# Three expert chunks moved from the recurrence to the heads of the first sequence's attention

## The chip, the cores and the metric

The kernel runs on one core of a Trainium2 chip. Five engines matter here: TensorE (PE) does matrix products and transposes, VectorE (DVE), ScalarE (ACT, activation functions and copies) and GpSimd (POOL) do elementwise work, and SyncE issues transfers. The metric is the time of one execution in device microseconds. The kernel before takes 3566.51 us, the median of three runs (3561.74 to 3568.43).

## The reference, cut to what matters

A small language model tower over 16 sequences of 256 tokens, width 256. Two layers, each an attention-like part and an expert part. Layer 0: token embedding, a linear recurrence with a channel mix, then a mixture of eight experts. Layer 1, where the change lies:

```
# recurrence (per channel, over time)
k = x @ Wk.T; r = x @ Wr.T; v = r
q = max(pp, u + k); y = (exp(pp-q)*a + exp(u+k-q)*v) / (exp(pp-q)*b + exp(u+k-q))
h = h + (sigmoid(r) * y) @ Wo.T
# attention, 16 heads of 16, causal, then four experts
h = rms(x) ; q, k, v = heads(h @ wq.T), ... ; attn = softmax(mask(q k^T / 4))
x = x + (attn v) @ wo.T            # first 64 columns set to zero
xf = rms(x); wts = top-2 of softmax(xf @ gate_w.T)
o0 = gelu(xf @ e0_up.T) @ e0_down.T
o1 = silu(xf @ e1_w1.T) * (xf @ e1_w2.T) @ e1_down.T
o2 = gelu(gelu(gelu(xf @ e2_l1.T) @ e2_l2.T) @ e2_l3.T) @ e2_l4.T
o3 = gelu(gelu(xf @ e3_down.T) @ e3_up.T) @ e3_out.T
out = x + sum of wts[e] * o_e      # first 64 columns set to zero
```

## The kernel before, in words

Three phases follow each other: a (layer 0's embedding and recurrence), b (layer 0's experts) and c (layer 1). Only phase c is touched. It works on eight tiles of 512 tokens, two sequences each. Values that need more than bf16 are split into a high and a low bf16 half, and each product is three passes (high by high, low weight by high, high by low).

Each engine has a queue that runs in order. All four compute engines walk the same list of steps, `ORDER_C`, and each engine does its own part of a step; semaphores connect the parts. The *front* of a tile is:

- f2, the key and receptance products of the recurrence, and their copies on ScalarE; r2, the end of the router of the tile before, on VectorE.
- A0/A1: VectorE makes the exponents of channel half 0 or 1. R0/R1: ScalarE takes the exponentials (L1276), VectorE runs the scans and the division (L1461 to L1483). Z0/Z1: ScalarE writes the high half of the result z (L1287), VectorE the low half (L1490).
- f5: TensorE's output product (first row L1739, after z), VectorE's addition and statistics, GpSimd's reciprocal roots (L1204 to L1208). g5: VectorE applies the normalization (L1398). f6: TensorE transposes, ScalarE and GpSimd split.
- Q0 to Q3, K0 to K3, T0 to T3: the q, k, v products, their norms, and the transposed stacks (L1801). M0/M1: maxima of the scores per sequence; N0/N1: their negative, transposed (L1325).
- S0 to S15 and V0 to V15: the heads of the first sequence. S: TensorE's scores (L1846 to L1850) into one of two banks, ScalarE's exponential (L1333), VectorE's high half (L1580), and the low half on GpSimd (L1223) or, for every third head, on VectorE (L1583). V: TensorE's weighted values (L1867 to L1870). V of a head stands three heads behind its S; the weights have four buffers (PB). S16 to V31 are the second sequence. O0/O1: ScalarE copies the result (L1340).

The *back* of a tile is its router and its experts, cut into 42 chunks: in the order of `WORK`, four each of e2_l1, e0_up, e2_l2 and e0_down, two of e3_down, four each of e2_l3, e3_up, e2_l4, the gated expert e1, e3_out and e1_down. An *up* chunk is six matmuls of 512 columns (contraction 256) or twelve (contraction 512, as e2_l2 and e2_l3), two gelus on ScalarE (L1367, L1368) and one low half on GpSimd (L1233). It may start when the gelus of the up chunk two before it are done (`free`). A *down* chunk is twelve matmuls of 192 columns (L1956) and, for the last of four, an update of h on VectorE (L1716). A number in `ORDER_C` stands for that many chunks, the next in line, and `heads_order(b, fill)` puts `fill[h]` chunks behind head h.

The experts of tile t run in the same walk as the front of tile t+1. So the first tile's front runs without chunks, seven walks have both (`Fori` holds five of them), and the last tile's experts run alone.

ScalarE's functions come in table sets. Where the function of the next activation is in another set than the last, the program has an ACT_TABLE_LOAD before it; gelu is in another set than the exponential, copies load nothing.

Of the kernel before, what the change touches and what calls it, by code (L numbers as in the profile page):

```python
# [935 lines left out]
def heads_order(b, fill, lag=3):  # L936

    steps = []
    for h in range(HEADS + lag):
        if h < HEADS:  # L940
            steps.append("S%d" % (b * HEADS + h))
        if h >= lag:
            steps.append("V%d" % (b * HEADS + h - lag))
        if h in fill:
            steps.append(str(fill[h]))
    return " ".join(steps)


ORDER_C = " ".join((
    "f2 A0 r2 R0 A1 8 Z0 1 R1 6 Z1 f5 3 g5 2 f6 1 Q0 Q1 K0 2 T0 K1 1 T1 1 M0 1 N0",  # L950
    heads_order(0, {8: 1}), "O0",
    "Q2 3 Q3 K2 1 T2 K3 1 T3 1 M1 1 N1",
    heads_order(1, {4: 1, 9: 1, 14: 1}), "O1 1 f13 f0 1 g13 b0 1 g0 1 y0 1 b1 f1 r1"))

# [1114 lines left out]
```

## Time and profile before

| | |
|---|---|
| median of three runs | 3566.51 us (3561.74 to 3568.43) |
| the profiled execution, its time | 3563.41 us |
| its span, first to last instruction | 3561.6 us |
| busy in the span: TensorE | 2902.6 us (81%) |
| VectorE | 2051.2 us (58%) |
| ScalarE | 1674.7 us (47%) |
| GpSimd | 791.4 us (22%) |
| mean granted TensorE clock | 0.919 |

The profile is of one execution. Its page cuts the span into 40 slices; phase c fills the last 19 of them, where the TensorE digits are 6 to 8 and ScalarE's 3 to 5. The timeline lists instructions with start, duration, engine, line and what they write and read. A bracket at its end says how long the engine had been idle, and whose instruction ended the wait. The names `c_...` are tiles of phase c; `xT_hi` and `xT_lo` are memory of an earlier phase that phase c uses for its own buffers (in the heads `xT_lo` holds the weights in f32 and `xT_hi` their halves). A granted clock of 1.00 is 2.4 GHz, 0.50 is 1.2 GHz.

### The profile page before, as it was taken

How to read it: one execution, taken by the hardware profiler on the slowest of the kernel's cores; microseconds unless marked ns; L12 is line 12 of the kernel's file. 1: busy time of each engine (PE TensorE's matmuls, PEld its weight loads, DVE VectorE, ACT ScalarE, POOL GpSimd, SP SyncE). 2: the span in 40 equal slices, each digit the busy share in tenths (PEclk: the TensorE clock that was granted, in tenths of full speed). 3: DMA queues.
4: the chain of work that ended last, by engine and by line, in shares of the span. 5: the costliest groups of instructions: out<-in, count | busy, mean ns of one | idle time of the engine just before them, and what ended most of it. 6: DMA issues, size and time to landing. Idle time of an engine off the chain costs nothing. (4 is left out here: it accounts for less than half of the span.)

```text
span 3561.6 us, 59951 instructions
## 1 busy us (share of the span) xinstructions
PE 2902.6 (81%) x21952; PEld 1880.1 (53%) x21952; DVE 2051.2 (58%) x3989; ACT 1674.7 (47%) x2804; POOL 791.4 (22%) x813
## 2 busy tenths in 40 slices
PE   4877759999999999999994667777777777777778
PEld 2544446666666666666662444445353444445354
DVE  6777734444444444444446576665766676675762
ACT  2544535555555555555442445443544545453543
POOL 4545320000000000000000143432333243333333
PEclk8989879999999999999997789998998988898999
DMA  1000010000000000000000000000000000000000
GB/s 60 7 12 12 1 48 23 21 20 18 18 18 21 19 18 18 18 22 18 0 0 0 1 1 1 7 1 8 1 1 7 1 7 1 7 1 7 1 1 13
DMA packets 17448, 40.58 MB, mean 11 GB/s; under 512 B 2944, under 2 KB 7040, under 8 KB 17152
## 3 DMA queue, kind: packets, MB, share of 16 engines
q1 hardware_dynamic: 15744, 34.11, 3.1%
q0 software_dynamic: 1536, 4.20, 0.4%
q8 instruction: 110, 1.80, 0.2%
q14 instruction: 58, 0.48, 0.0%
HBM read 34.10 MB, written 4.19 MB: 11 GB/s over the span
## 5 line engine op out<-in xcount | busy, mean ns | idle before, releaser
L864 DVE TENSOR_TENSOR b_glo<-b_f,b_ghi 128x512 bf16<-128x512 f32 x512 | 354.1, 692 | 715.5 <-ACT b_ghi L807 715.4
L806 ACT ACTIVATE b_f<-b_up,b_b 128x512 f32<-128x512 f32 x512 | 352.5, 688 | 609.7 <-PE b_up L901 583.3
L915 PE MATMUL b_down<-b_W_hi,b_ghi 128*128 128x256 bf16 x2048 | 558.4, 273 | 17.4 <-DVE b_glo L864 17.4
L915 PE MATMUL b_down<-b_W_lo,b_ghi 128*128 128x256 bf16 x2048 | 558.2, 273 | 0.0
L915 PE MATMUL b_down<-b_W_hi,b_glo 128*128 128x256 bf16 x2048 | 558.2, 273 | 0.0
L1233 POOL TENSOR_TENSOR c_hid_lo<-c_g,c_hid_hi 128x512 bf16<-128x512 f32 x208 | 266.1, 1289 | 673.2 <-ACT c_hid_hi L1368 395.3
L807 ACT ACTIVATE b_ghi<-b_up,b_b 128x512 bf16<-128x512 f32 x512 | 349.2, 682 | 0.0
L901 PE MATMUL b_up<-xT_hi,b_W_hi 128*128 x1024 | 305.4, 380 | 13.1 <-DVE b_W_lo L819 13.1
L1190 POOL TENSOR_TENSOR c_frs<-c_fmv,eps 128x4 f32<-128x4 f32 x8 | 1.6, 197 | 1394.1 <-DVE c_fmv L1391 1394.1
L901 PE MATMUL b_up<-xT_hi,b_W_lo 128*128 x1024 | 305.1, 380 | 0.0
L901 PE MATMUL b_up<-xT_lo,b_W_hi 128*128 x1024 | 305.0, 379 | 0.0
L915 PEld LDWEIGHTS b_down<-b_W_hi,b_ghi 128*128 128x128 bf16 x2048 | 200.3, 98 | 92.6 <-issue 35.1
L915 PEld LDWEIGHTS b_down<-b_W_lo,b_ghi 128*128 128x128 bf16 x2048 | 200.4, 98 | 58.0
L915 PEld LDWEIGHTS b_down<-b_W_hi,b_glo 128*128 128x128 bf16 x2048 | 200.4, 98 | 23.2
L1367 ACT ACTIVATE c_g<-c_back 128x512 f32<-128x512 f32 x176 | 105.1, 597 | 216.6 <-PE c_back L1732 186.8
L1223 POOL TENSOR_TENSOR xT_hi<-xT_lo,xT_hi 128x384 bf16<-128x384 f32 x176 | 170.1, 978 | 158.6 <-DVE xT_hi L1580 158.6
L1333 ACT ACTIVATE xT_lo<-c_front 128x384 f32<-128x384 f32 x256 | 123.7, 491 | 113.3 <-PE c_front L1850 98.4
L901 PEld LDWEIGHTS b_up<-xT_hi,b_W_lo 128*128 128x128 bf16 x1024 | 100.4, 98 | 121.4 <-issue 1.0
L901 PEld LDWEIGHTS b_up<-xT_lo,b_W_hi 128*128 128x128 bf16 x1024 | 100.3, 98 | 121.1 <-issue 0.6
L1580 DVE CAST xT_hi<-xT_lo 128x384 bf16<-128x384 f32 x256 | 106.6, 435 | 87.1 <-ACT xT_lo L1333 83.9
L1560 DVE TENSOR_REDUCE c_mx<-c_front 128x2 f32<-128x512 f32 (+1 forms) x192 | 125.3, 688 | 47.1 <-PE c_front L1822 42.4
L1739 PE MATMUL c_front<-WC_hi,c_xhi 128*128 128x256 bf16 (+2 forms) x256 | 68.7, 359 | 97.7 <-DVE c_xlo L1490 33.7
(351 smaller groups left out, 6764.9 us busy)
## 6 DMA issues: line engine op xcount, KB each, us to landing
b_stage<-in_WP SPq DMA_DIRECT2D x59, 383.0 KB, 3.1
out<-h SPq DMA_DIRECT2D x8, 512.0 KB, 2.9
xT_hi<-in_WA SPq DMA_DIRECT2D x4, 512.0 KB, 6.0
xT_lo<-in_WA SPq DMA_DIRECT2D x3, 512.0 KB, 9.2
b_b<-in_b SPq DMA_DIRECT2D x1, 1024.0 KB, 5.2
b_ghi<-in_WP SPq DMA_DIRECT2D x2, 383.0 KB, 6.7
b_glo<-in_WP SPq DMA_DIRECT2D x2, 383.0 KB, 6.9
a_emb<-in_emb,idx POOLq DMA_INDIRECT x32, 2.8
```

What stands on the lines that cost most here:

```text
L806: act.activation(f[:, k % 4, :], ub[k % 4][:, :], ACT.Gelu, bias=b1[par][:, k:k + 1])
L807: act.activation(ghi[:, k, :], ub[k % 4][:, :], ACT.Gelu, bias=b1[par][:, k:k + 1]).then_inc(g_hi.sem, 1)
L864: dve.tensor_tensor(glo[:, k, :], f[:, k % 4, :], ghi[:, k, :], ALU.subtract).then_inc(g_lo.sem, 1)
L901: m = pe.matmul(ub[k % 4][:, :], wp[par][:, q * H0 + k * P:q * H0 + (k + 1) * P], xp[:, bass.ds(t * TT + q * N, TT)], start=(n == 0 and q ...
L915: m = pe.matmul(ob[s // 2][:, (s % 2) * D:(s % 2 + 1) * D], xp[:, k, s * P:(s + 1) * P], wp[par][:, w], start=(k == 0 and n == 0 and s % 2 ...
L1223: pool.tensor_tensor(pl[:, n % PB, :], pf[:, n % PB, :], ph[:, n % PB, :], ALU.subtract).then_inc(p_lo_pool.sem, 1)
L1233: pool.tensor_tensor(hid_lo[dst][:, k, :], g[:, h % 2, :], hid_hi[dst][:, k, :], ALU.subtract).then_inc(lo_ready.sem, 1)
L1333: act.activation(pf[:, n % PB, :], fb[n % 2][:, 0:3 * P], ACT.Exp).then_inc(p_f.sem, 1)
L1367: act.activation(g[:, h % 2, :], bb[2 + u % 2][:, :], ACT.Gelu)
L1560: dve.tensor_reduce(o, fb[n % 2][:, :].rearrange("p (h k) -> p h k", k=w), AX.X, ALU.max).then_inc(mx_ready.sem, 1)
L1580: dve.tensor_copy(ph[:, n % PB, :], pf[:, n % PB, :]).then_inc(p_hi.sem, 1)
L1739: m = pe.matmul(o, xs[xp][:, k, s * P:(s + 1) * P], W(WC[wp], name, k, 0, n), start=(j == 0 and k == 0), stop=(j == 2 and k == KC - 1))
```

## The change

The number of chunks before Z0 goes from eight to five, and the first sequence's heads have four places for a chunk instead of one. The chunks keep their own order, so each chunk from the sixth to the twenty-seventh comes three places later.

```diff
-    "f2 A0 r2 R0 A1 8 Z0 1 R1 6 Z1 f5 3 g5 2 f6 1 Q0 Q1 K0 2 T0 K1 1 T1 1 M0 1 N0",
-    heads_order(0, {8: 1}), "O0",
+    "f2 A0 r2 R0 A1 5 Z0 1 R1 6 Z1 f5 3 g5 2 f6 1 Q0 Q1 K0 2 T0 K1 1 T1 1 M0 1 N0",
+    heads_order(0, {3: 1, 7: 1, 11: 1, 15: 1}), "O0",
```

Written out with the chunks' names, before and after:

| place | before | after |
|---|---|---|
| before Z0 | e2_l1 x4, e0_up x4 | e2_l1 x4, e0_up x1 |
| Z0 to R1 | e2_l2 | e0_up |
| R1 to Z1 | e2_l2 x3, e0_down x3 | e0_up x2, e2_l2 x4 |
| f5 to g5 | e0_down, e3_down x2 | e0_down x3 |
| g5 to f6 | e2_l3 x2 | e0_down, e3_down |
| f6 to Q0 | e2_l3 | e3_down |
| K0 to T0 | e2_l3, e3_up | e2_l3 x2 |
| K1 to N0 | e3_up x3 | e2_l3 x2, e3_up |
| heads, first sequence | e2_l4 | e3_up x3, e2_l4 |

On ScalarE, from the negated maxima (L1325) through the heads of the first sequence up to the third group of exponentials (L1333), with the gelus of a chunk (L1367, L1368):

```order
 L1325 ACTIVATE c_negT<-c_front 128x256
 L1333 ACT_TABLE_LOAD
-L1333 ACTIVATE xT_lo<-c_front 128x384 x16
+L1333 ACTIVATE xT_lo<-c_front 128x384 x4
+L1367 ACT_TABLE_LOAD
+L1367 ACTIVATE c_g<-c_back 128x512
+L1368 ACTIVATE c_hid_hi<-c_back 128x512
+L1333 ACT_TABLE_LOAD
+L1333 ACTIVATE xT_lo<-c_front 128x384 x4
```

The sixteen exponentials stood in one row; now a gelu pair with a table load on either side stands behind the fourth, and in the same way behind the eighth and the twelfth.

On ScalarE, at the end of the recurrence, the gelus (L1367, L1368) that stand ahead of the high half of z (L1287) of channel half 1:

```order
 L1368 ACTIVATE c_hid_hi<-c_back 128x512
+L1367 ACTIVATE c_g<-c_back 128x512
+L1368 ACTIVATE c_hid_hi<-c_back 128x512
+L1367 ACTIVATE c_g<-c_back 128x512
+L1368 ACTIVATE c_hid_hi<-c_back 128x512
+L1367 ACTIVATE c_g<-c_back 128x512
+L1368 ACTIVATE c_hid_hi<-c_back 128x512
 L1287 ACTIVATE c_xhi<-xT_lo 128x512
```

Three gelu pairs stood between the exponentials of that half and z; now it is six.

On GpSimd, from the reciprocal root of the second normalization (L1208) to the low halves of its transposed rows (L1214), with the low halves of chunks (L1233):

```order
 L1208 TENSOR_TENSOR c_frs<-c_frs 128x4
-L1233 TENSOR_TENSOR c_hid_lo<-c_g,c_hid_hi 128x512 x4
+L1233 TENSOR_TENSOR c_hid_lo<-c_g,c_hid_hi 128x512
 L1214 TENSOR_TENSOR c_xlo<-xT_hi,c_xhi 128x512 x2
```

Four low halves of chunks stood there, and one does now.

## Rows read from the trace of the kernel before

**Rows 1.** Four stretches: PE, PEld, DVE, ACT, POOL busy, clock, DMA, GB/s.
```profile
2294.70:2496.30 201.60, 149.36 (x1288) 93.49 (x1288) 136.07 (x272) 92.72 (x159) 70.92 (x69) 0.89 0.01 4
2384.80:2402.70 17.90, 13.73 (x252) 11.60 (x252) 12.15 (x21) 9.04 (x18) 11.42 (x12) 0.97 0.01 2
2334.80:2340.00 5.20, 5.14 (x25) 3.70 (x26) 0.69 (x1) 0.00 (x0) 0.00 (x0) 0.50 0.00 0
2370.80:2374.20 3.40, 3.40 (x17) 1.71 (x15) 0.00 (x0) 2.94 (x3) 0.76 (x1) 0.50 0.00 0
```

**Rows 2.** ScalarE timeline, heads of the first sequence: start, busy us, what.
```profile
2384.77 1.28 ACT L1333 ACT_TABLE_LOAD   x1
2386.06 0.87 ACT L1333 ACTIVATE xT_lo<-c_front 128x384 f32<-128x384 f32 x2
2388.96 0.49 ACT L1333 ACTIVATE xT_lo<-c_front 128x384 f32<-128x384 f32 x1 [0.76 <-PE c_front L1850]
2392.93 0.49 ACT L1333 ACTIVATE xT_lo<-c_front 128x384 f32<-128x384 f32 x1 [0.50 <-PE c_front L1850]
2396.59 0.49 ACT L1333 ACTIVATE xT_lo<-c_front 128x384 f32<-128x384 f32 x1 [0.18 <-PE c_front L1850]
2402.61 0.69 ACT L1340 ACTIVATE xT_lo<-c_front 128x272 f32<-128x272 f32 x2 [2.72 <-PE c_front L1870]
```

**Rows 3.** GpSimd timeline: the first low half of the heads.
```profile
2387.03 0.92 POOL L1223 TENSOR_TENSOR xT_hi<-xT_lo,xT_hi 128x384 bf16<-128x384 f32 x1 [1.32 <-DVE xT_hi L1580]
```

**Rows 4.** TensorE timeline: first matmul after the first values.
```profile
2388.24 0.27 PE L1846 MATMUL c_front<-xT_hi,c_kz 128*128 128x256 bf16 x1
```

**Rows 5.** ScalarE timeline: a load and the two gelus of a chunk.
```profile
2363.02 1.28 ACT L1367 ACT_TABLE_LOAD   x1 [0.64 <-PE c_back L1732]
2364.32 0.60 ACT L1367 ACTIVATE c_g<-c_back 128x512 f32<-128x512 f32 x1
2364.81 0.59 ACT L1368 ACTIVATE c_hid_hi<-c_back 128x512 bf16<-128x512 f32 x1
```

**Rows 6.** TensorE timeline: a chunk of six matmuls, and what follows it.
```profile
2366.15 0.59 PE L1732 MATMUL c_back<-c_hid_hi,WC_hi 128*128 128x512 bf16 x2
2370.34 0.66 PE L1801 MATMUL c_front<-identb,c_qs 128*128 128x128 bf16 x8 [2.74 <-DVE c_qs L1545]
```

**Rows 7.** TensorE timeline: last pair of matmuls of another such chunk.
```profile
2382.68 0.59 PE L1732 MATMUL c_back<-c_hid_lo,WC_hi 128*128 128x512 bf16 x2
```

**Rows 8.** ScalarE timeline: the first gelu of that chunk.
```profile
2383.39 0.60 ACT L1367 ACTIVATE c_g<-c_back 128x512 f32<-128x512 f32 x1 [7.82 <-PE c_back L1732]
```

**Rows 9.** TensorE timeline in the recurrence, second half.
```profile
2309.16 1.04 PE L1732 MATMUL c_back<-c_hid_hi,WC_hi 128*128 128x512 bf16 x4
2311.76 1.03 PE L1732 MATMUL c_back<-c_hid_hi,WC_hi 128*128 128x512 bf16 x4
2323.45 1.89 PE L1732 MATMUL c_back<-c_hid_hi,WC_hi 128*128 128x512 bf16 x4 [5.62 <-ACT c_hid_hi L1368]
2327.50 0.25 PE L1956 MATMUL c_back<-WC_hi,c_hid_hi 128*128 128x192 bf16 x1
2334.86 0.59 PE L1739 MATMUL c_front<-WC_hi,c_xhi 128*128 128x256 bf16 x2 [4.23 <-ACT c_xhi L1287]
```

**Rows 10.** ScalarE timeline there: exponentials, and the high half of z.
```profile
2318.99 2.00 ACT L1276 ACTIVATE xT_lo<-xT_lo 128x1024 f32<-128x1024 f32 x2 [2.68 <-DVE xT_lo L1453]
2333.40 0.63 ACT L1287 ACTIVATE c_xhi<-xT_lo 128x512 bf16<-128x512 f32 x1 [4.54 <-DVE xT_lo L1483]
```

**Rows 11.** VectorE timeline there: the low half of z.
```profile
2334.07 0.69 DVE L1490 TENSOR_TENSOR c_xlo<-xT_lo,c_xhi 128x512 bf16<-128x512 f32 x1 [0.69 <-ACT c_xhi L1287]
```

**Rows 12.** VectorE timeline: the normalization applied, at two places.
```profile
2275.81 1.38 DVE L1398 TENSOR_SCALAR c_xn<-h,c_fmv,c_frs 128x256 f32<-128x256 f32 x4
2346.55 3.89 DVE L1398 TENSOR_SCALAR c_xn<-h,c_fmv,c_frs 128x256 f32 x4 [2.28 <-POOL c_frs L1208]
```

**Rows 13.** GpSimd timeline beside the second of them.
```profile
2346.47 3.50 POOL L1233 TENSOR_TENSOR c_hid_lo<-c_g,c_hid_hi 128x512 bf16<-128x512 f32 x3
```

## The prediction

> **What bounds the kernel now.** I read the activity slices of the page first: the second half of the run, from about 1,900 us on, is the last phase, and there no engine is full. Then I cut that phase into turns of its pipeline. The page's table of stretches shows the turn from 2294.70 to 2496.30 [rows 1]: 201.6 us, in which TensorE is busy 149 us, VectorE 136, ScalarE 93 and GpSimd 71. So a turn is a chain of dependent steps across engines, not the load of one engine, and what counts is which wait ends last at each place. Seven turns run expert chunks of one tile beside the recurrence and attention of the next, and the change is in all seven; the phases before it and the last tile's experts, which run alone, stay as they are.
>
> Two places matter. In the **recurrence**, TensorE waits 5.62 us and then 4.23 us [rows 9]: VectorE's chain sets the end, and z's high half (ScalarE) and low half (VectorE) release the output product at 2334.86 [rows 9 to 11]. In the **heads of the first sequence**, 17.9 us per turn, ScalarE is busy 9.04 us, so it idles 8.86 [rows 1]. The exponentials of heads 4, 8 and 12 start at 2388.96, 2392.93 and 2396.59 [rows 2]: four heads take 3.97 and 3.66 us. The cycle of exponential, high half, low half and values sets this pace, with work of up to four heads buffered.
>
> **What is moved.** Three chunks fewer stand before Z0, so every later chunk up to the first of the second sequence slides by three. The recurrence loses three down chunks (matmuls alone). What reaches the heads is the last three chunks of e3_up and, as before, one down chunk. An e3_up chunk costs TensorE six matmuls, ScalarE two gelus and GpSimd one low half, and its gelus stand between exponentials. The order listing shows a table load before each gelu pair and another before the next exponential.
>
> **Heads, term 1: the three stalls.** A chunk of six matmuls starts at 2366.15 and is over at 2370.34 minus 2.74, 2367.60: 1.45 us [rows 6]. ScalarE starts 0.12 us after such an end (2382.68 + 0.59, then 2383.39) [rows 7, 8]. A load takes 1.30 us from start to start, and the two gelus end 1.08 us after they start (2364.32 to 2364.81 + 0.59) [rows 5]. The load back takes 1.29 us (2384.77 to 2386.06) [rows 2]. So between chunk and next exponential lie 0.12 + 1.30 + 1.08 + 1.29 = 3.79 us.
> - First stall: TensorE comes to the chunk after the values of head 0, at 2388.24 [rows 4]. The exponential of head 4 starts at 2388.24 + 1.45 + 3.79 = 2393.48, not 2388.96: +4.5 us.
> - Then a cycle: from the exponential of head 4 to the end of its values. For head 0 this was 2386.06 to 2388.24, 2.18 us, with the low half from 2387.03 inside [rows 2 to 4]. The next chunk stands behind those values. Cycle: 2.18 + 1.45 + 3.79 = 7.42 us for four heads, where 3.97 and 3.66 stood: +3.4 and +3.8 us.
> - Tail: from head 12 to the copy of the output took 6.02 us (2396.59 to 2402.61) [rows 2]. The pipe is now empty when head 12 starts. I take 2.18 us for its values and the average pace of (3.97 + 3.66)/8 = 0.95 us for three more heads, 5.0, and add 0.4 for the down chunk: −0.6 us.
>
> Sum +11.1 us a turn. GpSimd's extra low half (3.50/3 = 1.17 us [rows 13]) falls into the load back plus the next exponential and high half, where GpSimd waits anyway; if that cover were gone it would add its 1.2 us per chunk. The bounds: if buffers hid all they can, the load on ScalarE is the floor. 9.04 + 3 × (1.30 + 1.08 + 1.29) = 20.05 us against 17.9, so +2.1. Above, with each stall fully added: 3 × (1.45 + 3.79) = +15.7. I take 11.1, as the places in the order leave TensorE only one or two scores to run ahead.
>
> The Trainium skill, "ScalarE: Activation LUTs", section "What ACT_TABLE_LOAD costs", says that a switch costs 1.283 us for the load and about 1.38 us more for a drain. The rows show 1.28 us of load and the next activation 1.29 to 1.30 us after its start, with no drain behind it [rows 2, 5]. By the page the six switches would cost 8.3 us more a turn; I keep the rows' price.
>
> **Heads, term 2: the clock.** Each stall leaves TensorE without work for some 3 us. After an idle time of 2.74 us [rows 6] the granted clock was 0.50, that is 1.2 GHz, in the next 3.4 us, and after 4.23 us [rows 9] it was 0.50 for 5.2 us [rows 1]. At that level a chunk's matmuls (1.45 us, 1.3 of it streaming) take 1.3 us more. Not every stall need meet it: 0 to 3 × 1.6 us. I take +1.0.
>
> **Recurrence, term 3.** ScalarE has five chunks before z's first half, one between, and now six gelu chunks, not three, between the second exponentials and z's second half (listing). A chunk with contraction 512 takes 2.60 us (2309.16 to 2311.76), and the first after the long wait 4.05 (2323.45 to 2327.50) [rows 9]. TensorE may run only two ahead of the gelus, so four such chunks wait for the second exponentials. The first starts at about 2323.45 as now, the fourth ends 4.05 + 3 × 2.60 = 11.85 later, 2335.3, plus 0.2 of latency and 0.12. The gelus end 1.08 later, about 2336.65. Only then does ScalarE write z's high half, which started at 2333.40 [rows 10]. From there to the output product it is 1.46 us, with the low half inside [rows 9 to 11]. So the product starts at 2338.1, not 2334.86: +3.3 us. It can be 0 if the clock recovers earlier and VectorE's chain stays last, and 5 if GpSimd's low halves, now during the end of that chain, slow it further.
>
> **After it, terms 4 to 6.** The product ran wholly at clock 0.50 for 5.2 us behind an idle 4.23 us [rows 1, 9]. The wait will be near 2.8 us, so part of it may run at 2.4 GHz, where it would take 2.6: 0 to −2.6, I take −1.2. The second normalization takes 3.89 us while GpSimd does three low halves in 3.50 us, where four tiles take 1.38 us undisturbed [rows 12, 13]. VectorE and GpSimd hold each other up: 2.51 us for three. One low half is left there: −1.5 us (0 to −2.5). But TensorE has about 4 us less of matmuls there (three chunks of 2.60 us give way to shorter ones), so the transposes and q, k, v products may be granted 1.2 GHz: 0 to +3, I take +1.0. The chunks between q, k, v and the maxima change size by 1.3 us each, beside VectorE steps: +0.2. The down update that now stands behind the normalization has 5 us of VectorE's waiting to lie in: 0.
>
> **Sum.** 11.1 + 1.0 + 3.3 − 1.2 − 1.5 + 1.0 + 0.2 = +13.9 us a turn, seven turns: +97 us. The profiled execution took 3563.4 us (span 3561.6 and 1.8 around it), 0.09% under the median of 3566.5. 3563.4 + 97 = 3660 us.
>
> **Rivals.**
> - *The heads absorb the loads, and the front gains.* ScalarE idles half of the heads, TensorE's gaps there are filled, and the product after the recurrence comes no later and warm. It decides if the heads cost just their floor. 2.1 − 2.6 − 1.5 = −2.0 a turn, 3549 us, faster. For it: four buffers. Against it: two score banks, so ScalarE's pause stops TensorE after at most two scores. 3%.
> - *The heads pay, the recurrence does not.* VectorE's chain still ends last and the product runs warm: 11.1 + 0 − 2.6 − 1.5 = 7.0, 3612 us. 13%.
> - *The clock falls in every stall.* 11.1 + 4.8 + 3.3 − 0 − 1.5 + 3 = 20.7, 3708 us. 9%.
> - *A drain behind each switch.* ScalarE's pipe has to empty at a switch inside a dense row of exponentials, at the price of a second load each, 6 × 1.28 = 7.7 us a turn: 21.6, 3715 us. Against it: both loads in the rows are followed at once by the activation. 2%. "ScalarE: Activation LUTs" of the Trainium skill has such a drain.
> - *No effect*, since other waits cover it: against it, that nothing catches up later in a chain of steps. 1%.
>
> The forecast holds 72%. The range of 3605 to 3705 us reaches from the second rival to near the third. About 0.2% (7 us) is what a measurement here can tell from no change. Faster 3%, same 1%, slower 96%.
>
> **What would show it.** ScalarE's table loads in the last phase: 42 more (six in each of seven turns). In the heads, idle of 1.5 us before a load behind TensorE's e3_up matmuls, exponentials in groups of four some 7.4 us apart, and the stretch from the negated maxima to the output copy at 29 us, not 17.9. In the recurrence, the high half of z waits for the gelus, not for VectorE. The second normalization takes near 2.4 us. I am wrong if the groups are under 5 us apart, if z's high half still waits for VectorE, or if the turn grows by less than 6 us.

## The result, and the profile after

The changed kernel takes 3650.82 us, the median of four runs (3648.22 to 3653.70); the kernel before took 3567.35 beside it, also over four. The ratio is 1.0237, with an interval of 1.0220 to 1.0255. The medians are 83.5 us apart. The profiled execution has a span of 3650.8 us where it was 3561.6: +89.2 us; the stages below are read from these two.

Two lines of the page after: the span, and the busy times of TensorE and ScalarE (busy us, share, instructions).

```profile
span 3650.8 us, 59993 instructions
PE 2910.8 (80%) x21952; PEld 1890.8 (52%) x21952; DVE 2037.1 (56%) x3989; ACT 1723.9 (47%) x2846; POOL 789.3 (22%) x813
```

ScalarE's count grew from 2804 to 2846: the 42 instructions are the table loads. Its busy time grew by 49 us, so busy time alone is at most a little over half of the loss.

I cut phase c into the same stages in both traces, by landmarks on the engines. These are us per turn: first the turn that starts at 2294.8 before and at 2305.5 after, one of the five that the loop runs, then the first turn, which is written out.

| stage | loop, before | after | written out, before | after |
|---|---|---|---|---|
| exponentials of half 0 to those of half 1 (L1276) | 24.23 | 24.23 | 24.14 | 24.15 |
| to z's high half (L1287) | 14.41 | 17.51 | 14.32 | 17.56 |
| to the last addition of f5 (L1497) | 6.90 | 4.93 | 6.77 | 4.81 |
| to the normalization (L1398) | 6.25 | 6.26 | 6.26 | 6.25 |
| to the q, k norms (L1518) | 12.02 | 10.55 | 12.00 | 10.27 |
| to the negated maxima (L1325) | 25.79 | 25.61 | 25.48 | 25.36 |
| **heads**, to the output copy (L1340) | 18.25 | 32.70 | 18.21 | 26.79 |
| to the second sequence's negated maxima | 40.44 | 38.78 | 40.05 | 39.00 |
| its heads | 18.34 | 18.34 | 18.31 | 18.32 |
| to the next turn | 34.99 | 36.26 | 32.46 | 32.42 |
| turn | 201.62 | 215.17 | 198.00 | 204.93 |

The other loop turns grew by 12.5, 14.3, 14.0 and 16.9 us, the last turn by 7.2. With 0.5 for the turn without chunks and 3.3 us by which phase c started later this is the 89.2. (The later start is no effect of the change: in the profiled executions of the seven experiments phase c starts anywhere between 1916.5 and 1920.3.)

The turn of the table is typical for the heads, less so for the rest. Over all seven turns the heads lost 88.4 us, the recurrence (to z, to f5, and from the normalization to the norms, together) 3.3, and the last stage 6.1; the stage behind the heads gained 11.5. In the recurrence the seven turns go from −0.45 to +3.8 us, the last number in the fifth turn of the loop.

The same stretches of after as in [rows 1], columns as there: the loop turn, its heads, the heads of the written-out turn, and the output product after the recurrence.

```profile
2305.50:2520.60 215.10, 149.69 (x1288) 95.08 (x1288) 133.73 (x271) 99.93 (x165) 70.56 (x69) 0.87 0.01 4
2395.00:2427.20 32.20, 22.24 (x270) 16.25 (x270) 11.38 (x21) 19.58 (x29) 14.72 (x15) 0.79 0.00 1
2191.90:2218.70 26.80, 18.83 (x261) 13.78 (x259) 11.95 (x23) 18.46 (x29) 13.84 (x14) 0.92 0.01 1
2347.90:2353.00 5.10, 3.79 (x39) 3.55 (x40) 2.71 (x5) 0.00 (x0) 0.66 (x1) 1.00 0.00 0
```

TensorE is busy 149.7 us a turn, as before. The heads were 17.9 us at a granted clock of 0.97; in the loop they are now 32.2 at 0.79, in the written-out turn 26.8 at 0.92. The output product went from 0.50 to 1.00.

ScalarE's timeline of the loop turn's heads in the kernel after (start, busy us, what; the bracket is the wait), which answers to [rows 2]:

```profile
2394.98 1.28 ACT L1333 ACT_TABLE_LOAD   x1
2396.27 0.87 ACT L1333 ACTIVATE xT_lo<-c_front 128x384 f32<-128x384 f32 x2
...
2400.00 1.28 ACT L1367 ACT_TABLE_LOAD   x1 [1.60 <-PE c_back L1732]
2401.29 0.60 ACT L1367 ACTIVATE c_g<-c_back 128x512 f32<-128x512 f32 x1
...
2402.39 1.28 ACT L1333 ACT_TABLE_LOAD   x1
2403.69 0.87 ACT L1333 ACTIVATE xT_lo<-c_front 128x384 f32<-128x384 f32 x2
...
2408.86 1.28 ACT L1367 ACT_TABLE_LOAD   x1 [2.71 <-PE c_back L1732]
...
2412.55 0.87 ACT L1333 ACTIVATE xT_lo<-c_front 128x384 f32<-128x384 f32 x2
...
2418.12 1.28 ACT L1367 ACT_TABLE_LOAD   x1 [2.29 <-PE c_back L1732]
...
2421.82 0.87 ACT L1333 ACTIVATE xT_lo<-c_front 128x384 f32<-128x384 f32 x2
...
2427.27 0.69 ACT L1340 ACTIVATE xT_lo<-c_front 128x272 f32<-128x272 f32 x2 [2.20 <-PE c_front L1870]
```

ScalarE waits for the chunk's matmuls, and only then starts the load. Groups of four heads start at 2396.27, 2403.69, 2412.55 and 2421.82. TensorE's timeline of the same heads: the three e3_up chunks (a row is a pair of matmuls), and what released TensorE after each.

```profile
2398.44 0.59 PE L1732 MATMUL c_back<-c_hid_hi,WC_hi 128*128 128x512 bf16 x2
...
2404.23 0.28 PE L1846 MATMUL c_front<-xT_hi,c_kz 128*128 128x256 bf16 x1 [3.01 <-ACT xT_lo L1333]
...
2406.04 1.01 PE L1732 MATMUL c_back<-c_hid_hi,WC_hi 128*128 128x512 bf16 x2
2406.84 1.06 PE L1732 MATMUL c_back<-c_hid_hi,WC_lo 128*128 128x512 bf16 x2
2407.70 1.06 PE L1732 MATMUL c_back<-c_hid_lo,WC_hi 128*128 128x512 bf16 x2
...
2413.09 0.40 PE L1846 MATMUL c_front<-xT_hi,c_kz 128*128 128x256 bf16 x1 [2.94 <-ACT xT_lo L1333]
...
2415.30 1.01 PE L1732 MATMUL c_back<-c_hid_hi,WC_hi 128*128 128x512 bf16 x2
```

It idles 3.01, 2.94 and 2.58 us behind the three chunks, and the chunk that follows the first or the second idle time runs at 1.2 GHz: from its first pair to the matmul behind it are 2.51 us (2406.04 to 2408.55), where the first chunk had 1.29 (2398.44 to 2399.73).

Now ScalarE in the heads of the first, written-out turn of after:

```profile
2191.85 0.93 ACT L1333 ACTIVATE xT_lo<-c_front 128x384 f32<-128x384 f32 x2 [0.33 <-PE c_front L1850]
2192.80 1.28 ACT L1367 ACT_TABLE_LOAD   x1
2194.55 0.60 ACT L1367 ACTIVATE c_g<-c_back 128x512 f32<-128x512 f32 x1 [0.47 <-PE c_back L1732]
...
2196.94 0.87 ACT L1333 ACTIVATE xT_lo<-c_front 128x384 f32<-128x384 f32 x2
...
2203.24 0.87 ACT L1333 ACTIVATE xT_lo<-c_front 128x384 f32<-128x384 f32 x2
...
2210.48 0.87 ACT L1333 ACTIVATE xT_lo<-c_front 128x384 f32<-128x384 f32 x2
```

Here the load starts at once behind the exponentials, beside TensorE's chunk, and the wait of 0.47 us stands on the gelu. The cycles are 6.30 and 7.24 us, not 8.86 and 9.27. TensorE idles 1.66 us in each, and its clock falls once, from 2204.0 to 2207.4 in the 7.24. The reason for the shorter cycles lies in ScalarE's order in the kernel after, with its waits. The first line of each pair is what carries the wait for the chunk's matmuls (`c_up_ps`):

```
written out:  L1367 ACT_TABLE_LOAD [waits c_lo_ready]
              L1367 ACTIVATE c_g<-c_back 128x512 [waits c_up_ps]
in the loop:  L1366 REGISTER_ALU [waits c_up_ps]
              L1367 ACT_TABLE_LOAD
              L1367 ACTIVATE c_g<-c_back 128x512 [waits c_lo_ready]
```

The program waits for `up_ps` and then for `lo_ready`. In the loop the values waited for are held in registers, and the first wait became an instruction of its own ahead of the load. Written out, it is the activation that waits.

In the recurrence of the loop turn, ScalarE after ([rows 10]), then VectorE ([rows 11, 12]), TensorE ([rows 9]) and GpSimd ([rows 13]):

```profile
2329.71 2.00 ACT L1276 ACTIVATE xT_lo<-xT_lo 128x1024 f32<-128x1024 f32 x2 [2.68 <-DVE xT_lo L1453]
...
2338.48 0.60 ACT L1367 ACTIVATE c_g<-c_back 128x512 f32<-128x512 f32 x1 [3.38 <-PE c_back L1732]
...
2346.25 0.60 ACT L1367 ACTIVATE c_g<-c_back 128x512 f32<-128x512 f32 x1 [1.50 <-PE c_back L1732]
...
2347.22 0.63 ACT L1287 ACTIVATE c_xhi<-xT_lo 128x512 bf16<-128x512 f32 x1
```

```profile
2343.96 0.69 DVE L1483 SCALAR_TENSOR_TENSOR xT_lo<-xT_hi,xT_lo 128x512 f32<-128x512 f32 x1
2347.88 1.23 DVE L1490 TENSOR_TENSOR c_xlo<-xT_lo,c_xhi 128x512 bf16<-128x512 f32 x1 [3.23 <-ACT c_xhi L1287]
...
2358.41 2.22 DVE L1398 TENSOR_SCALAR c_xn<-h,c_fmv,c_frs 128x256 f32 x4 [3.59 <-POOL c_frs L1208]
```

```profile
2334.17 1.89 PE L1732 MATMUL c_back<-c_hid_hi,WC_hi 128*128 128x512 bf16 x4 [5.64 <-ACT c_hid_hi L1368]
...
2349.21 0.38 PE L1739 MATMUL c_front<-WC_hi,c_xhi 128*128 128x256 bf16 x2 [3.08 <-issue]
```

```profile
2358.52 1.31 POOL L1233 TENSOR_TENSOR c_hid_lo<-c_g,c_hid_hi 128x512 bf16<-128x512 f32 x1 [0.15 <-ACT c_hid_hi L1368]
```

VectorE has z ready at 2344.65, and ScalarE's high half comes at 2347.22, without a bracket, straight behind the last of six gelu pairs. In [rows 10] it had waited 4.54 us for VectorE. VectorE now waits 3.23 us for ScalarE.

### The profile page after: what moved, and what is told of

Read it like the earlier page. It is cut to its first block and busy times, and to the rows that moved or that the text cites. A ratio compares the mean times of both kernels' runs of the same rounds, so it can differ in the third digit from the quotient of the medians.

```text
span 3650.8 us, 59993 instructions
## 1 busy us (share of the span) xinstructions
PE 2910.8 (80%) x21952; PEld 1890.8 (52%) x21952; DVE 2037.1 (56%) x3989; ACT 1723.9 (47%) x2846; POOL 789.3 (22%) x813
## 5 line engine op out<-in xcount | busy, mean ns | idle before, releaser
L915 PE MATMUL b_down<-b_W_hi,b_ghi 128*128 128x256 bf16 x2048 | 558.4, 273 | 16.9 <-DVE b_glo L864 16.8
L1233 POOL TENSOR_TENSOR c_hid_lo<-c_g,c_hid_hi 128x512 bf16<-128x512 f32 x208 | 264.3, 1276 | 763.7 <-ACT c_hid_hi L1368 498.2
L1367 ACT ACTIVATE c_g<-c_back 128x512 f32<-128x512 f32 x176 | 105.1, 597 | 232.5 <-PE c_back L1732 229.8
L1580 DVE CAST xT_hi<-xT_lo 128x384 bf16<-128x384 f32 x256 | 114.1, 458 | 179.5 <-ACT xT_lo L1333 176.2
L1846 PE MATMUL c_front<-xT_hi,c_kz 128*128 128x256 bf16 (+1 forms) x512 | 132.8, 262 | 79.2 <-ACT xT_lo L1333 59.9
L1732 PE MATMUL c_back<-c_yhi,WC_hi 128*128 128x512 bf16 x288 | 99.7, 432 | 96.3 <-ACT c_hid_hi L1368 84.9
L1333 ACT ACTIVATE xT_lo<-c_front 128x384 f32<-128x384 f32 x256 | 121.3, 490 | 94.4 <-PE c_front L1850 82.6
```

Of the source, the lines that this page charges most:

```text
L915: m = pe.matmul(ob[s // 2][:, (s % 2) * D:(s % 2 + 1) * D], xp[:, k, s * P:(s + 1) * P], wp[par][:, w], start=(k == 0 and n == 0 and s % 2 ...
L1233: pool.tensor_tensor(hid_lo[dst][:, k, :], g[:, h % 2, :], hid_hi[dst][:, k, :], ALU.subtract).then_inc(lo_ready.sem, 1)
L1333: act.activation(pf[:, n % PB, :], fb[n % 2][:, 0:3 * P], ACT.Exp).then_inc(p_f.sem, 1)
L1367: act.activation(g[:, h % 2, :], bb[2 + u % 2][:, :], ACT.Gelu)
L1580: dve.tensor_copy(ph[:, n % PB, :], pf[:, n % PB, :]).then_inc(p_hi.sem, 1)
L1732: m = pe.matmul(bank[:, :], W(WC[wp], name, k, e * P, P), xs[xp][:, k, :], start=(j == 0 and k == 0), stop=(j == 2 and k == kc - 1))
```

## The experiments

**Each half of the change alone.** The change moves chunks out of the recurrence and into the heads. The first two kernels do one and leave the other, with the chunks taken from, or given to, the steps between q, k, v and the maxima.

```diff
 # e1: eight chunks stay before Z0
-    "... 8 Z0 1 R1 6 Z1 ... K0 2 T0 K1 1 T1 1 M0 1 N0", heads_order(0, {8: 1}), "O0",
+    "... 8 Z0 1 R1 6 Z1 ... K0 1 T0 K1 T1 M0 1 N0", heads_order(0, {3: 1, 7: 1, 11: 1, 15: 1}), "O0",
 # e2: five chunks before Z0, one in the heads
-    "... 8 Z0 1 R1 6 Z1 ... K0 2 T0 K1 1 T1 1 M0 1 N0",
+    "... 5 Z0 1 R1 6 Z1 ... K0 2 T0 K1 2 T1 2 M0 2 N0",
```

> The heads part of the change alone: the recurrence keeps its eight chunks before Z0, the four places in the first sequence's heads are filled as in the change (three chunks of e3_up, one down chunk), and the three come from the places between K0 and N0. Theory (ScalarE's table switches and gelus stall the row of exponentials): the stretch from the negated maxima to the output copy is 32.7 us in the turns of the loop and 26.8 in the first and last turn, as in the changed kernel, and the total is near it: 5 x 14.4 + 2 x 8.6 = 89, less about 1 us a turn between K0 and N0, so 3640 to 3655 us, ratio to before 1.021 to 1.026. Rival (the recurrence's delay is most of the cost): the heads stay below 25 us and the ratio below 1.010.

e1 took 3648.57 us, ratio 1.0239 [1.0222, 1.0256], as much as the whole change. Its loop heads took 30.1 to 32.5 us and its written-out ones 26.8, and the recurrence's stages were those of before (14.41, 6.8, 12.02). The stage that gave the three chunks, from the norms to the negated maxima, did not get shorter, as had been expected: it went from 25.79 to 26.00.

> The recurrence part alone: five chunks before Z0, one down chunk in the heads as in the kernel before, and the three chunks of e3_up go one each to K1, T1 and M0. Theory: from the second exponentials to the high half of z +3.1 us a turn, from there to the second addition to h -1.9, from the normalization to the first q, k norms -1.5, so the recurrence part adds up to nearly nothing (-0.5 a turn); the three chunks add 0 to 1.3 us each between K1 and N0. Heads 18.2 us. Ratio 1.000 to 1.006. Rival (the recurrence's delay costs its 3 us and nothing comes back): ratio 1.008 or more.

e2 took 3593.13 us, ratio 1.0082 [1.0065, 1.0098], above what was expected. In the recurrence its stages are those of after: 14.41 to 17.5, 6.9 to 4.93, 12.02 to 10.5, together −0.3 us in the first turn of the loop and, over all seven turns, +0.1 us. The heads stayed at 18.2. What costs is the stage that took the three chunks in, from the norms to the negated maxima: 25.79 to 28.58 in the loop, 25.48 to 29.16 written out, 2.8 and 3.7 us where 0 to 3.9 had been expected. These 21 us are most of the 28.5 by which the profiled execution is longer; another 2.0 is a later start of phase c, and this is how the ratio came out above its range. That stage's three chunks are no part of the change, so the two readings agree: the loss is the heads', and the recurrence comes out near even.

**Down chunks in place of up chunks.** The kernel before, with four chunks in the heads, all of them e2_l4, which give ScalarE nothing to do. The three extra ones come from the second sequence's first step.

```diff
-    heads_order(0, {8: 1}), "O0",
-    "Q2 3 Q3 K2 1 T2 K3 1 T3 1 M1 1 N1",
+    heads_order(0, {3: 1, 7: 1, 11: 1, 15: 1}), "O0",
+    "Q2 Q3 K2 1 T2 K3 1 T3 1 M1 1 N1",
```

> The same four places in the heads, but filled with the four down chunks of e2_l4, which have matmuls alone and nothing on ScalarE or GpSimd; the recurrence as before, and the three that stood between Q2 and Q3 are gone from there. Theory: heads stay at 17.9 to 19.5 us, since TensorE has room there and ScalarE is not switched; between Q2 and Q3 up to 2.5 us are saved, ratio 0.994 to 1.000. Rival (any chunk between the heads costs its own TensorE time and more, as it delays scores and values): heads at 21 us or more, ratio 1.000 to 1.006.

e3 took 3559.81 us over ten runs (3557.5 to 3564.3), ratio 0.9985 [0.9975, 0.9994]. The heads took 19.0 us, +0.8, for as many chunks at the same places. So neither the number of chunks nor their places cost the time, but what an e3_up chunk has and a down chunk has not: gelus and table loads on ScalarE, a low half on GpSimd, and matmuls of 512 columns. What e3 wins, it wins in the two written-out turns: the stage behind the heads is 35.6 us where it was 40.0, and the first turn 194.46 instead of 198.00. In the loop that stage is 2.0 to 3.1 us shorter, and 0.8 in the heads and 1.1 to 1.5 before the next turn take this back. It is the fastest version of the study, if by less than a measurement here can surely tell (0.2%).

**No switch.** The kernel after, with tanh, which shares the exponential's table set, in place of gelu in the three e3_up chunks of the heads; it computes another function there.

```diff
-   act.activation(g[:, h % 2, :], bb[2 + u % 2][:, :], ACT.Gelu)
+   fn = ACT.Tanh if name == "e3_up" and k > 0 else ACT.Gelu
+   act.activation(g[:, h % 2, :], bb[2 + u % 2][:, :], fn)
```

> The changed kernel with the function of the three chunks that stand in the heads, e3_up 1 to 3, replaced by tanh, which shares its table with the exponential, so that this part of the result is another function of the same size. The six table loads a turn go, all else stays. Theory: between a chunk's end and the next exponential only 0.12 + 1.08 us are left; groups of four heads at 4.9 us, heads at 20.5 to 22.5 us in all turns, ratio to before 1.002 to 1.008. Rival (the chunks' work on TensorE, ScalarE and GpSimd costs it, not the loads): heads stay above 26 us, ratio above 1.015.

e4 took 3588.91 us, ratio 1.0071 [1.0054, 1.0088]. ScalarE in its loop heads, behind the first chunk:

```profile
2389.55 0.60 ACT L1368 ACTIVATE c_g<-c_back 128x512 f32<-128x512 f32 x1 [1.61 <-PE c_back L1733]
...
2390.52 0.88 ACT L1333 ACTIVATE xT_lo<-c_front 128x384 f32<-128x384 f32 x2
...
2395.96 0.88 ACT L1333 ACTIVATE xT_lo<-c_front 128x384 f32<-128x384 f32 x2
...
2400.95 0.88 ACT L1333 ACTIVATE xT_lo<-c_front 128x384 f32<-128x384 f32 x2
```

The groups are 5.44 and 4.99 us apart, and the heads take 22.6 us in the loop, 22.8 written out. The row of those in the loop, in the stretch table, has the clock at 1.00 throughout:

```profile
2384.20:2406.70 22.50, 17.24 (x270) 13.40 (x270) 14.14 (x21) 11.88 (x25) 15.04 (x15) 1.00 0.01 2
```

Of the 14.45 us that the heads lost in the loop, 10.1 go with the six loads (six by 1.28 us are 7.7; the other 2.4 are about what two chunks at 1.2 GHz cost, 1.2 us each). Written out it is 4.0 of 8.6. What is left, 4.4 to 4.6 us, comes with the rest of these chunks: exponentials that stand behind gelus which wait for TensorE, GpSimd's low halves, and the longer matmuls. No run takes these apart.

**The load beside the chunk, in the loop too.** The kernel after, with the two waits of a gelu exchanged where the turn is the loop's. Then the load need not wait for the matmuls.

```diff
-   act.wait_ge(up_ps.sem, up_ps.at(t, u + 1))
-   act.wait_ge(lo_ready.sem, lo_ready.at(t, max(h - 1, 0)))
+   waits = [(up_ps, u + 1), (lo_ready, max(h - 1, 0))]
+   for which, at in waits if isinstance(t, int) else waits[::-1]:
+       act.wait_ge(which.sem, which.at(t, at))
```

> The changed kernel with the two waits before a gelu pair in the other order inside the loop: first for the low halves (long done), then for TensorE's chunk. The second wait sits on the activation itself, so the table load ahead of it no longer waits for the chunk, as in the first and last turn, which are written out. Theory: the difference of 5.9 us between a turn of the loop and the first or last turn is the load that stands behind the chunk there, with the lower clock that the longer stall brings. The heads of the loop's turns fall from 32.7 to 26 to 28 us, the first and last stay at 26.8, total 5 x 5 to 6 us less, 3620 to 3628 us, ratio 1.014 to 1.018. Rival (the loop's register instructions or the place in the program make it slower): heads stay above 30 us, ratio above 1.020.

e5 took 3608.53 us, ratio 1.0128 [1.0113, 1.0143], a little under what was expected: half of the loss is gone by the order of two waits. The exchange reaches every gelu pair of the loop, but of the 44.7 us between the profiled executions of after and e5, 33.9 are in the loop's heads (3.6 are the start of phase c). ScalarE in its loop heads:

```profile
2394.58 1.28 ACT L1368 ACT_TABLE_LOAD   x1
2396.09 0.60 ACT L1368 ACTIVATE c_g<-c_back 128x512 f32<-128x512 f32 x1 [0.23 <-PE c_back L1733]
...
2398.49 0.87 ACT L1333 ACTIVATE xT_lo<-c_front 128x384 f32<-128x384 f32 x2
...
2404.71 0.87 ACT L1333 ACTIVATE xT_lo<-c_front 128x384 f32<-128x384 f32 x2
...
2410.86 0.87 ACT L1333 ACTIVATE xT_lo<-c_front 128x384 f32<-128x384 f32 x2
```

The load stands behind the exponentials, as in the written-out turn of after, and the cycles are 6.22 and 6.15 us. One row of the stretch table (e5, loop heads) has the clock:

```profile
2391.00:2416.60 25.60, 18.16 (x270) 14.48 (x270) 11.51 (x21) 20.28 (x32) 15.28 (x15) 0.93 0.01 2
```

With the load hidden the clock is 0.93, not 0.79. The loop heads take 25.3 to 26.8 us, those written out 26.8 as before. So the difference between the two kinds of turn was the place of the load, with the lower clock that came with it.

**The same exchange without the change.** e6 is the kernel before with these two waits exchanged, e7 is e3 with them. Both ask if the exchange is a gain in itself.

> The kernel before with the same order of waits in the loop. No gelu stands in its heads, so by the theory they stay at 18.2 us; one load a turn, behind the second q, k, v product, can start up to 1.3 us earlier, of which ScalarE's work on the stacks gets at most a part. Ratio 0.998 to 1.000. Rival (the order of waits helps in general, by more than the heads): ratio below 0.995.

> The down chunks in the heads (e3) with the loads early (e6). If the two gains add, ratio 0.996 to 0.999, heads 19.0 us. If the clock after the heads, which cost e3 1.3 us a turn, falls otherwise, the ratio may be 1.000.

e6 took 3575.38 us, ratio 1.0028 [1.0018, 1.0039], e7 3575.04 over twelve runs (3560.18 to 3608.84), ratio 1.0028 [1.0009, 1.0048]. Both are slower by 0.3%, which no theory had; both expectations missed. In e6 the heads stay at 18.2 to 18.6. The 12.0 us by which its profiled execution is longer are scattered: 2.8 lie ahead of phase c, 3.7 go with a longer second normalization in three of the five loop turns, 4.4 come before the next turn in two of them, and the rest is in several places. One of the three turns with the longer normalization won 2.4 us ahead of it and was no slower in all. VectorE and GpSimd of one of them:

```profile
2349.52 4.92 DVE L1399 TENSOR_SCALAR c_xn<-h,c_fmv,c_frs 128x256 f32 x4 [2.30 <-POOL c_frs L1208]
```

```profile
2349.44 4.86 POOL L1233 TENSOR_TENSOR c_hid_lo<-c_g,c_hid_hi 128x512 bf16<-128x512 f32 x4
```

Before, GpSimd did three low halves in a row there, then had a gap, and the normalization took 3.89 us [rows 12, 13]. With four in a row it takes 4.92, and in e7 4.91 in four of five loop turns. In the turn shown, the exchange brought the last of these four gelu pairs 0.2 us closer to the third (1.28 us apart, where it was 1.52), and the gap shrank from 0.36 to 0.12 us. Why the exchange moved them so, and the 2 us before the next turn, stay open.

## Why the prediction was right

3660 us were forecast, 3650.82 came (+97 forecast, +83.5 between the medians), and the forecast's mechanism is the one that the experiments show: ScalarE's gelus and table loads break the row of exponentials. By its steps, in us per loop turn, forecast and measured:

| step | forecast | loop | written out |
|---|---|---|---|
| first stall | +4.5 | +4.52 | +3.24 |
| second and third group | +3.4, +3.8 | +4.89, +5.60 | +2.58, +3.57 |
| tail | −0.6 | −0.57 | −0.83 |
| clock in the heads | +1.0 | in the groups | in the groups |
| heads together | +12.1 | +14.45 | +8.58 |
| output product later | +3.3 | +3.6 | |
| the product at the higher clock | −1.2 | −2.5 | |
| to the last addition, both together | +2.1 | +1.13 | +1.28 |
| normalization | −1.5 | −1.67 | −1.73 |
| q, k, v and the maxima | +1.2 | 0.0 | −0.1 |
| behind the heads | 0 | −0.4 | −1.1 |
| turn | +13.9 | +13.55 | +6.9 |

- **Heads, term 1.** Right in mechanism and, for the first stall and the tail, to 0.1 us: 2403.69 − 2396.27 is 7.42, the cycle that the sum had worked out, against 2.90 in [rows 2]. e1 shows that it is the heads, e3 that it is not the number or the places of the chunks, and e4 that the table switches are 10.1 of the 14.45 us and 4.4 remain without them.
- **Heads, term 2, the clock.** Too small for the loop. The second and the third chunk both ran at 1.2 GHz, 1.2 us more each, and scores and values behind them were slower too: the two groups took 8.86 and 9.27 us, 1.44 and 1.85 over the 7.42, 3.3 us together. The +1.0 is what failed; the bound of +4.8 held it. The 1.6 us per stall behind that bound had no row, and these two come out near it.
- **What the sum missed: the two kinds of turn.** It put the load behind the chunk in all seven turns. In the two written-out ones it runs beside it, and the heads lost 8.6, not 12.1. The order of the waits on ScalarE shows it, and I had read the order without its waits. The two errors have opposite signs, and so the total is nearer than its parts: the heads' term is 2.35 us too small in a loop turn and 3.5 too large in a written-out one. That a loop turn came so near, 13.55 against 13.9, is luck in part: the +1.2 for q, k, v and the maxima did not come, and the recurrence up to the last addition cost 1.0 less than its +2.1, which offset the heads.
- **Recurrence, term 3.** From the exponentials to the product it was 15.87 us and is 19.50, +3.6 where +3.3 stood. z waits for the gelus, whose pairs come 2.59 us apart. The low half took 1.23 us instead of 0.69, which I had not counted; a GpSimd low half (2347.41 to 2348.56) runs beside it.
- **Terms 4 and 5.** The product ran wholly at 2.4 GHz behind a wait of 3.08 us, so its gain was the whole bound in this turn. From its start to the last addition it was 5.44 us and is 2.94. Not every turn gained it: from z to the last addition the fourth and fifth turns of the loop took 5.7 before, and 4.9 and 6.4 after. The normalization takes 2.22 us beside one low half, near the 2.4 forecast.
- **Term 6.** The +1.0 for q, k and v didn't come. Only the transposes before them (1.72 us for eight where 1.09 had stood) and one chunk were slow; from 2365.0 to 2376.0 us the granted clock is 1.00.
- **Not foreseen**: behind the heads the clock is in another phase. In the ten us after them TensorE's granted clock was 0.72 and is 1.00, and the stage is 1.66 us shorter. Behind the second sequence's heads it is the other way round: the transposes take 1.09 us where they took 1.97, but the product after them 0.53 us a pair where it took 0.33, and the next turn starts 1.27 us later. TensorE's rows of after:

```profile
2486.32 1.09 PE L1746 MATMUL c_front<-ident,c_xn 128*128 128x128 f32 x8 [0.95 <-DVE c_xn L1594]
...
2490.78 0.53 PE L1739 MATMUL c_front<-WC_lo,c_xhi 128*128 128x192 bf16 x2
```

e3, which puts no load into the heads, shows the second shift too (+1.5); its −2.0 behind the heads is another matter, as three chunks have left that stage and its clock in the ten us behind the heads is 0.66. e4, with after's chunks and without the loads, has −0.65 and +0.05. What makes TensorE's clock fall at one of these places and not at the other stays open.

Of the rivals, *the heads pay, the recurrence does not* is out for its condition, since z does wait for the gelus; but its low price for the recurrence was nearly right, as that came out at −0.3 us in the turn of the table and +3.3 over all seven. *The clock falls in every stall* holds in the loop's heads, where the clock was 0.50 from 2405.4 to 2408.8, 2412.2 to 2419.0 and 2422.4 to 2425.8, behind each of the three idle times; written out it fell behind one of three, and the product after the recurrence ran at 1.00. *The heads absorb the loads* is out by the 14.45. *A drain behind each switch*, with which the Trainium skill's "ScalarE: Activation LUTs", section "What ACT_TABLE_LOAD costs", agrees, is out: in the rows of the loop's heads each activation starts 1.29 or 1.30 us after its load's start, which is the load of 1.28 and nothing more, and the load back starts at 2402.39, 0.02 us behind the gelu before it (2401.78 + 0.59). Where an activation starts later (2194.55, 2396.09), its bracket names TensorE's chunk.

## What to carry to other kernels

Work that fills one engine's gaps is to be priced on every engine that it touches: the same four places in the heads cost 0.8 us in a loop turn with chunks of matmuls alone, and 14.4 with three chunks among them that make ScalarE change its table set twice each. A table load hides only if nothing ahead of it waits for the data; look at which instruction carries the wait, in the loop and outside it apart. And where VectorE and GpSimd work side by side, a shift of 0.2 us went with a closed gap and one more us, so an edit that looks free has to be timed.

## What the runs showed of the hardware

- Where it waits for nothing else, the activation behind a table load starts 0.01 to 0.02 us after the load's end, for gelu and the exponential.
- The same normalization of four tiles on VectorE (L1398) took 1.38 us without a low half on GpSimd beside it [rows 12], 2.22 with one, 3.89 with three and a gap, and 4.92 with four in a row. GpSimd's low half took 1.31 us in after and 1.17 on average in the row of three [rows 13]. Tile by tile, an instruction of VectorE took 0.40 or 0.41 us alone; beside a low half it took 1.22 to 1.35 and ended 0.14 or 0.15 us after it, in all eight cases looked at (three in the turn of before, one in after, four in e6). The third of before, VectorE and GpSimd:

```profile
2348.86 1.26 DVE L1398 TENSOR_SCALAR c_xn<-h,c_fmv,c_frs 128x256 f32 x1
```

```profile
2348.82 1.15 POOL L1233 TENSOR_TENSOR c_hid_lo<-c_g,c_hid_hi 128x512 bf16<-128x512 f32 x1
```

- Behind an idle time of TensorE of 3.08 us the product ran at a granted clock of 1.00, behind one of 4.23 us at 0.50 [rows 1, 9]. In the heads, waits of 3.01 and 2.94 us between short pieces of work were followed by 1.2 GHz, and not at once: the first scores after 3.01 us took 0.28 us each, and only the chunk 1.8 us later was slow. In the written-out turn idle times of 1.66 us were followed by 1.2 GHz once in three. So the length of the idle time alone does not tell what comes behind it.
